# Three-layer macaron kernel: fills of the key operands' extra rows moved from the set-up block into the layer loop, and the residual's tokens normalised later

## The reference

```python
x = x + 0.5 * _L0_ffn_ref(_layernorm(x, axis=-1), ...)
x = x + _L0_attn_ref(_layernorm(x, axis=-1), ...)
x = x + 0.5 * _L0_ffn_ref(_layernorm(x, axis=-1), ...)
```

```python
q, k = _rope(q, k)
scores = jnp.einsum('bqhd,bkhd->bhqk', q, k) / jnp.sqrt(jnp.float32(HD))
scores = jnp.where(causal[None, None], scores, jnp.finfo(scores.dtype).min)
attn = jax.nn.softmax(scores, axis=-1)
x = x + ao @ wo
```

## Time and profile before

| | |
|---|---|
| median of 3 runs | 1919.13 us |
| lowest and highest | 1913.59 and 1921.05 us |
| the profiled execution's own time | 1916.23 us |
| its span, first to last instruction | 1914.7 us |
| granted TensorE clock, mean | 0.91 of full speed |
| busy: PE, DVE, ACT, POOL | 1698.2, 1369.8, 1073.3, 445.3 us |

### The profile page before, as it was taken

One profiled execution on the slowest core, in us unless ns is written; L12 is line 12 of the kernel. 1 busy time (PEld: TensorE's weight loads), 2 busy tenths in 40 slices (PEclk: granted clock), 3 DMA queues, 4 the chain that ended last, 5 costly groups with the idle time before them and its releaser, 6 DMA issues. The chain is left out here.

```text
span 1914.7 us, 30151 instructions
## 1 busy us (share of the span) xinstructions
PE 1698.2 (89%) x10630; PEld 740.2 (39%) x10630; DVE 1369.8 (72%) x2705; ACT 1073.3 (56%) x2301; POOL 445.3 (23%) x491
## 2 busy tenths in 40 slices
PE   4899999999749947899999999579999999984895
PEld 2333333333247733233333342233333333324674
DVE  8788998986253338888999983388889998815333
ACT  3355777677604423356777678235576767771442
POOL 6300201111015647000102020260010100110564
PEclk9688999999859977889999999778899999995898
DMA  4500203300011135200202000242010020000113
GB/s 131 128 7 3 51 2 106 63 2 2 8 29 39 44 93 150 51 1 2 51 2 51 2 2 2 66 138 44 2 35 19 2 51 2 2 8 22 37 42 87
DMA packets 59432, 75.61 MB, mean 39 GB/s; under 512 B 9527, under 2 KB 52092, under 8 KB 57976
## 3 DMA queue, kind: packets, MB, share of 16 engines
q1 hardware_dynamic: 50056, 62.10, 12.6%
q0 software_dynamic: 4992, 9.32, 1.8%
q10 hardware_dynamic: 4224, 2.10, 0.4%
HBM read 52.97 MB, written 21.43 MB: 39 GB/s over the span
## 5 line engine op out<-in xcount | busy, mean ns | idle before, releaser
L747 ACT ACTIVATE probs<-ps 128x512 f32<-128x512 f32 (+3 forms) x1920 | 879.0, 543 | 471.7 <-PE ps L855 470.3
L598 DVE TENSOR_REDUCE mpart<-ps 128x1 f32<-128x512 f32 (+3 forms) x1680 | 1014.6, 665 | 115.9 <-PE ps L809 65.1
L809 PE MATMUL ps<-ka,qa 96*128 96x512 bf16 (+3 forms) x1920 | 670.3, 371 | 36.3 <-DMA ka<-ksplit 22.8
L855 PE MATMUL ps<-qa,ka 96*128 96x512 bf16 (+3 forms) x1920 | 617.0, 357 | 1.1 <-DMA qa<-guard 0.5
L868 PE MATMUL ps<-probs,vv 128*9 128x512 f32 (+3 forms) x3840 | 442.5, 533 | 8.8 <-ACT probs L747 8.1
L696 POOL TENSOR_SCALAR_AFFINE_SELECT probs<-probs 128x512 f32<-128x512 f32 x192 | 121.8, 634 | 1178.5 <-ACT probs L747 1178.5
L809 PEld LDWEIGHTS ps<-ka,qa 96*128 96x128 bf16 x1920 | 191.9, 101 | 480.2 <-DVE mpart L598 339.1
L855 PEld LDWEIGHTS ps<-qa,ka 96*128 96x128 bf16 x1920 | 183.7, 100 | 187.1 <-ACT probs L747 69.1
L812 PE MATMUL ps<-mask_rows,identb 128*128 128x128 bf16 x768 | 162.0, 236 | 0.0
L1189 DVE SCALAR_TENSOR_TENSOR probs<-probs,slot_w,ps 128x448 f32<-128x448 f32 x78 | 53.0, 680 | 120.0 <-PE ps L1118 120.0
L868 PEld LDWEIGHTS ps<-probs,vv 128*9 128x9 f32 x3840 | 57.8, 88 | 158.3 <-ACT probs L747 116.3
(11 more groups left out here) (163 smaller groups left out, 1070.6 us busy)
## 6 DMA issues: line engine op xcount, KB each, us to landing
qa<-qsplit SPq DMA_DIRECT2D x27, 384.0 KB
ka<-ksplit SPq DMA_DIRECT2D x27, 384.0 KB
probs<-rope SPq DMA_DIRECT2D x12, 512.0 KB, 6.8
qa<-qsplit SPq DMA_DIRECT2D x36, 96.0 KB
ka<-ksplit SPq DMA_DIRECT2D x36, 96.0 KB
qsplit<-arena SPq DMA_DIRECT2D x6, 384.0 KB, 3.2
ksplit<-arena SPq DMA_DIRECT2D x6, 384.0 KB, 2.8
tokens<-arena SPq DMA_DIRECT2D x2, 1024.0 KB, 5.1
```

Of the source, the lines that this page charges most:

```text
L598: dve.tensor_reduce(mpart[:, j % MD, h0:h0 + some, qt, kc], ps[:, bank, 0:some * w].rearrange("p (h w) -> p h w", h=some), axis=AX.X, op=A ...
L747: act.activation(probs[:, s % 2, h, 0:n], ps[:, u % SB, 0:n], ACT.Exp, scale=SCALE).then_inc(probs_ready, 1)
L809: ins = pe.matmul(dst, qa[0:KROWS, b, h0 + k, tile * 128:(tile + 1) * 128], ka[0:KROWS, b, h0 + k, kc * CH:kc * CH + n], start=True, stop= ...
L855: pe.matmul(dst, ka[0:KROWS, b, h, kt * 128:(kt + 1) * 128], qa[0:KROWS, b, h, c * CH + q0:(c + 1) * CH], start=True, stop=True).then_inc( ...
```

## The change

The two fills of `ka` leave the set-up block, one from GpSimd and one from VectorE. In the attention block of every layer GpSimd now fills `key_guard(0)` where it filled `guard_rows(1)`, and after the last `third` it fills `key_guard(1)` and `guard_rows(1)`. SP waits for the first of these fills ahead of its first load of operands. The 16 operations that write `x1` go from the place behind the last `third` to the start of chunk 3.

```diff
         @block.gpsimd
         def _(pool):
-            pool.memset(key_guard(1), ONES).then_inc(pool_s, 1)
-            pool.wait_ge(pool_s, 1)
-            n = 1
+            n = 0
...
             dve.memset(vv[:, :, :, :], 1.0).then_inc(dve_s, 1)
-
-            dve.memset(key_guard(0), ONES).then_inc(dve_s, 1)
...
+                    if c == 1:
+                        sp.wait_ge(keys_guarded, 1)
                     if c:
                         load_first(c - 1)
...
             @block.gpsimd
             def _(pool):
-                pool.memset(guard_rows(1), 0.0).then_inc(guard_zeroed, 1)
-                pool.wait_ge(guard_zeroed, 1)
+                pool.memset(key_guard(0), ONES).then_inc(keys_guarded, 1)
+                pool.wait_ge(keys_guarded, 1)
...
                 third(2 * NC - 1)
+                pool.wait_ge(part2_ready, 2 * NC)
+                pool.memset(key_guard(1), ONES).then_inc(keys_guarded, 1)
+                pool.wait_ge(keys_guarded, 2)
+                pool.memset(guard_rows(1), 0.0).then_inc(guard_zeroed, 1)
+                pool.wait_ge(guard_zeroed, 1)
+
                 for i in (3, 4):
                     pool.wait_ge(parts_stored[i % PB], stored(i))
                 pool.wait_ge(part2_ready, 2 * NC)
                 pool.wait_ge(roots_ready, 1)
-                for t in range(TT):
-                    pool.tensor_scalar(x1[:, t, :], xs[:, t, :], mv[:, t, 0:1], rst[:, 0, t:t + 1],
-                                       ALU.subtract, ALU.mult).then_inc(x1_ready, 1)
                 for ev in events:
                     if ev[0] == "scores":
                         _, s, j, kt, h = ev
+                        if j == NC - 1 and kt == 0 and h == 0:
+                            for t in range(TT):
+                                pool.tensor_scalar(x1[:, t, :], xs[:, t, :], mv[:, t, 0:1], rst[:, 0, t:t + 1],
+                                                   ALU.subtract, ALU.mult).then_inc(x1_ready, 1)
```

More of the change, by code:

```diff
@@ L292, in macaron_kernel @@
     guard_zeroed = sem("guard_zeroed")
+    keys_guarded = sem("keys_guarded")
     chunk_loaded = [sem(f"chunk_loaded{c}") for c in range(NC)]
@@ L455, in _ @@
                     dve.bn_aggr(mv[:, t, :], stats[:, t, :]).then_inc(dve_s, 1)
-            dve.wait_ge(dve_s, 2 + TT)
+            dve.wait_ge(dve_s, 1 + TT)
     nc.all_engine_barrier(sems_to_clear=all_sems)
```

## The result

| | before | changed |
|---|---|---|
| median, same chip, 21 runs each | 1917.20 us | 1912.24 us |
| lowest to highest | 1913.59 to 1923.58 | 1910.33 to 1918.77 |
| ratio to before, 95% interval | | 0.9974 [0.9966, 0.9982] |
| span of the profiled execution | 1914.7 | 1915.8 |

The change takes 5.0 us off, 0.26%, with an interval of 3.5 to 6.5 us. The forecast was 3.5 us, 1915.6 us in absolute time. The profiled execution of the changed kernel has a longer span than that of before, though the medians say the opposite.

What follows compares the result with a forecast made beforehand. The set-up block was taken as pure delay bounded by VectorE's end, the layer work as covered: −3.5 + 0 + 0 + 0 from the 1919.13 median gives 1915.6 us, bounds 1914.7 to 1920.4, with run spread 1909.5 to 1921.

Steps and rivals of the forecast that it cites:

- term 1: Set-up block: without the two fills the loop starts 3.50 us earlier, between 2.1 and 4.4.
- the gap of 0.91: Set-up block: VectorE's idle ahead of its second instruction; if it stays, statistics start at 4.24, without it at 3.36.
- loads served in turn: Set-up block: case in which the first quarter of the tokens is in by 3 to 4, against 5.6 if sharing bandwidth.
- the floor at 8.11: Set-up block: GpSimd's end without its fill, the limit if VectorE's statistics end at 8.16, a gain of 4.4.
- term 2: Start of a layer: nothing changes, as both kernels have one GpSimd fill there, costing about 2.3 us in layer 0.
- term 3: Behind the last `third` of each layer: two fills of 3.50 us are covered and cost 0, at most 1.4.
- my upper bound of 1.4: First `maxout`: cost over three layers if its first operation, L613, is held by the second fill.
- The cover: Behind the last `third`: slack of 10.6 us for masks, 24.5 for SyncE; without it fills cost up to 7.1 a layer.
- the next candidate: First `maxout`: L616, the SBUF operation after L613, starting at 754.20 in layer 1 as the second fill ends.
- term 4: Start of chunk 3: moved `x1` takes 12.6 us with 33 to 36 of cover; 0 net, 2 at most.
- One sign of the forecast: Layers 1 and 2: every distance within a layer stays as before to 0.5 us.
- My rival of the clock: First scores: if L613 is held, TensorE stays longer at its lower clock, some 5 us a layer, 1931; chance 0.03.

Runs made afterwards that it cites:

- experiment 4: The changed kernel with two more GpSimd fills behind the last `third` of each layer; ratio to before 1.0018.
- Experiment 1: The changed kernel with VectorE's fill of the key rows put back into the set-up block; ratio to before 1.0010.
- experiment 2: The changed kernel with GpSimd's fill put back into the set-up block, VectorE's still out; ratio to before 0.9994.
- experiment 7: The changed kernel with `key_guard(0)` filled once by ScalarE in the set-up block, not at each layer's start; 1909.05 us, ratio to before 0.9952.
- experiment 11: The changed kernel with the fill at a layer's start moved behind VectorE's 16 normalising operations; ratio to before 0.9972.
- experiment 5: The changed kernel again without any edit, on another chip, for a second trace; 1913.78 us, ratio to before 0.9974.
- experiment 6: The kernel before with only the 16 `x1` operations moved to the start of chunk 3; ratio to before 1.0004.
- experiment 3: The changed kernel with the `x1` operations back behind the fills, ahead of the first masks; ratio to before 1.0005.
- experiment 9: The changed kernel with six extra matmuls before chunk 1's maxima transpose and row-maxima matmuls doubled until chunk 1's first scores; ratio to before 0.9966.
- experiment 10: The changed kernel with both ScalarE's single set-up fill and the doubled row-maxima matmuls; 1924.09 us, ratio to before 0.9937.
- experiment 8: The changed kernel with extra unread matmuls in TensorE's waits in the first two chunks; ratio to before 1.0104.

## Why the prediction was right

**The set-up block (term 1).** The step held: the loop starts 3.79 earlier, where I took 3.50 between 2.1 and 4.4. The difference is in what starts the statistics. I had kept the gap of 0.91 behind the fill of `vv`; in fact they start 0.50 behind it, when the first quarter of the tokens lands. With the first quarter at 3.6 to 3.9 in every trace without VectorE's fill the time of landing is the one that the prediction gave for loads served in turn, but they are not served so. In experiment 4, where VectorE waits for the first two quarters (until 3.62 and 5.66), 0.42 MB had moved by the first landing and 1.04 MB by the second, of 0.26 MB in each quarter. So the loads overlap. In the other traces the first landing alone decided; in experiment 4 the second wait, 0.76 us, put the start of the loop to 10.90. That both engines had to lose their fill (experiments 1 and 2) was in the sum as the floor at 8.11.

**The start of a layer (term 2).** The hold of 3.46 is unchanged, and experiments 7 and 11 show its price: the square root starts 2.2 and 2.4 us earlier than in experiment 5, against "about 2.3".

**The two fills (term 3).** Nothing, as taken. Which of VectorE's copies can be held was the open point; experiment 4 settles it with 0.28 against up to 3.51 us, and my upper bound of 1.4, which rested on L613 being held, does not apply. The cover that it gave, 10.6 us for the masks and 24.5 for SyncE, is not the one that counts. The nearer limit is L615 (L616 before), which the prediction named as the next candidate and saw starting as the fill ends, but did not put in the sum: it started 0.28 us behind the end of the fill in layer 1 and 0.25 in layer 2. Nothing was lost, by a margin of a quarter of a microsecond that the prediction did not state.

**x1 (term 4).** Nothing that shows, as taken (experiment 6). What the prediction left out is that the move has a part in the result: without it the fills push `x1` into the first masks, for about 2 us a layer (experiment 3).

**The sum.** 3.5 forecast, 3.8 by the traces, 5.0 [3.5, 6.5] by the ratio. Experiment 1 finds nothing of the missing 1.2 in the layers, and 3.8 is within the intervals of both measurements. I take the rest for the measurement's spread; that two independent ratios both came out at 0.9974 keeps a small further gain possible, and this stays open.

In absolute time 1912.24 is 3.4 below the forecast of 1915.6. Of this, 1.9 come from the starting point: the median of three runs was 1919.13, and that of 21 is 1917.20. The stated range is also added up wrongly. The bounds 1914.7 and 1920.4 with −5.5 and +1.9 give 1909.2 to 1922.3, not 1909.5 to 1921. The measured time is inside both.

**What did not hold.** One sign of the forecast failed: that in layers 1 and 2 every distance is as before to 0.5 us. They differ by 1.0 and 1.5 up to the first evacuation, and by 2.2 to the second. The 2.2 are TensorE's clock and belong to no kernel; the others are unexplained. The last `third` of layer 0 came 3.16 and the first mask 3.34 earlier, instead of 3.5. My rival of the clock named the right resource for the wrong reason: the clock needs no held copy to fall, and its 2.2 us come and go with the change and without it. The times of single runs go with the mean granted clock: of the 21 runs of the changed kernel, the four slowest (1914.9 to 1918.8 us) have 0.906 to 0.910, the five fastest (1910.3 to 1911.0) 0.909 to 0.911. But the distance between the evacuations is not the whole source. In experiments 9 and 10 it no longer varies in the traces, and their six runs each still spread over 6.6 and 12.3 us, against 10.0 for the 21 of before.

## What to carry to other kernels

A set-up block that ends in a barrier costs what its last engine costs, so read when each engine comes to the barrier and take the work from all that are near the end; here either of them alone gave 0 to 0.9 of the 3.8 us. Before a fill moves into a loop, look not only at what the engine itself waits for, but at which VectorE operations it can hold, and at what it pushes behind it. And before comparing two traces in total, compare the same distance in every repetition: where a difference comes in one fixed step, in either kernel, read the granted clock of that stretch first. Here the step of 2.2 us was the clock and not the change.

## What the runs showed of the hardware

- A GpSimd fill held VectorE operations that go from SBUF to SBUF with one input, until the fill's end: 16 elements took 3.46 us beside a fill and 0.17 without (experiment 7), a copy of 128 up to 3.51 instead of 0.21 (experiment 4). One that reads PSUM took 0.28 in the middle of a fill, and the product of PSUM with an SBUF tile 0.73 to 0.75 with a fill beside it or not. The Trainium skill (GPSIMD Engine Reference, Specifications) names contention with VectorE instructions in a two-port mode or with two SBUF inputs, and by VectorE: DVE Perf Modes (Why PSUM operands drop a tier) an operand in PSUM rules the two-port mode out. These rows agree; that the hold lasts to the end of the fill is read from the rows.
- TensorE fell from 2.4 to 1.2 GHz after a stretch of 4 us in which it was busy for 2.14 by the trace, with no pause over 0.8 in it (experiment 8), and stayed up where the stretch ahead of chunk 1's scores was filled (experiment 9).
- ScalarE copied a broadcast column into 32x4096 float32 in 3.61 us, behind a table load of 1.28 (experiment 7), hardly more than the memset of GpSimd (3.50) or VectorE (3.47).
